# A GNN kernel on one core: GpSimd's descriptor carve-out in SBUF at half its size

## The reference

```python
edge_index = jnp.stack([src, dst])
x = _layernorm(x + _L0_gnn_ref(x, edge_index, edge_attr_4, edge_attr_8, 12500, ...), axis=-1)
x = _layernorm(x + _L1_gnn_ref(x, edge_index, edge_attr_3, ...), axis=-1)
```

## Time and profile before

| | |
|---|---|
| Median of three runs | 19,247.4 us |
| Range of the runs | 19,130.4 to 19,343.0 us |
| Profiled execution, its own time | 19,350.1 us |
| Its span (first to last instruction) | 19,348.1 us |
| Mean granted TensorE clock in it | 0.837 |
| TensorE busy | 15,636.7 us, 81% |
| VectorE busy | 12,827.1 us, 66% |
| GpSimd busy | 10,966.2 us, 57% |
| ScalarE busy | 2,132.7 us, 11% |

### The profile page before, as it was taken

One profiled execution on the slowest core, in us unless ns is written; L12 is line 12 of the kernel. 1 busy time (PEld: TensorE's weight loads), 2 busy tenths in 40 slices (PEclk: granted clock), 3 DMA queues, 4 the chain that ended last, 5 costly groups with the idle time before them and its releaser, 6 DMA issues.

```text
span 19348.1 us, 198105 instructions
## 1 busy us (share of the span) xinstructions
PE 15636.7 (81%) x63343; PEld 8350.6 (43%) x63343; DVE 12827.1 (66%) x19056; ACT 2132.7 (11%) x2833; POOL 10966.2 (57%) x11418
## 2 busy tenths in 40 slices
PE   6788888888897887888887888878887887888876
PEld 3333333333344444444444444444444444444443
DVE  4565566566566666766766677666766676666766
ACT  1111111111111000000000000000000000000001
POOL 5455555555545656665654566656655666665654
PEclk7666677666678999999998999898998999999998
DMA  1000000000001111111111111111111111111111
GB/s 35 13 15 14 15 15 15 14 15 15 14 14 29 20 19 20 20 21 20 21 20 27 20 20 21 20 20 20 21 20 27 20 21 20 21 20 19 21 20 26
DMA packets 918110, 382.41 MB, mean 20 GB/s; under 512 B 645444, under 2 KB 871770, under 8 KB 917790
## 3 DMA queue, kind: packets, MB, share of 16 engines
q0 software_dynamic: 367488, 201.16, 7.7%
q1 hardware_dynamic: 379914, 151.24, 3.3%
q10 hardware_dynamic: 170644, 29.29, 0.8%
HBM read 344.13 MB, written 36.68 MB: 20 GB/s over the span
## 4 chain that ended last, share of the span: by engine, by line
PE 35%; DVE 23%; another core or an unknown queue 20%; issue 18%; POOL 1%; ACT 1%; DMA 0%; DVEq 0%; ACTq 0%; SPq 0%; POOLq 0%
PE ps L1669 16%; PE ps L1566 5%; PE ps L1655 4%; DVE big L1290 3%; PE ps L1582 3%; DVE big L1344 3%; DVE xg L1348 3%; DVE big L1017 2%; DVE big L1335 2%; PE ps L1555 2%; DVE big L1133 2%; PE ps L1549 1%; POOL xg L601 1%; PE ps L1681 1%
## 5 line engine op out<-in xcount | busy, mean ns | idle before, releaser
L601 POOL DMA_INDIRECT xg<-x_rows,idx x8205 | 7886.5, 961 | 5274.4 <-issue 2319.1
L1669 PE MATMUL ps<-xw,big 128*128 128x512 f32 x14112 | 7086.0, 656 | 1640.3 <-DVE big L1344 1420.8
L1669 PEld LDWEIGHTS ps<-xw,big 128*128 128x128 f32 x14112 | 2855.6, 210 | 5150.7 <-issue 3654.6
L601 POOL DMA_INDIRECT xg<-in_x,idx x3125 | 2990.0, 957 | 2760.4 <-DVE big L1101 1785.5
L1344 DVE TENSOR_TENSOR big<-ps,col_hot 128x512 f32<-128x512 f32 x1176 | 810.0, 689 | 3775.2 <-remote 2023.6
L1655 PE MATMUL ps<-big 128*128 128x128 f32 x18816 | 2478.5, 284 | 326.1 <-issue 199.0
L1566 PE MATMUL ps<-w,big 65*128 65x256 f32 x6272 | 2462.8, 534 | 205.1 <-DVE big L1133 187.8
L1655 PEld LDWEIGHTS ps<-big 128*128 128x128 f32 x18816 | 2269.7, 196 | 494.4 <-issue 292.1
L836 ACT COPY big<-ps 128x1024 f32<-128x1024 f32 x1176 | 1189.2, 1013 | 11480.3 <-remote 5734.2
L1566 PEld LDWEIGHTS ps<-w,big 65*128 65x128 f32 x6272 | 1543.8, 264 | 1937.7 <-issue 1593.0
L1065 DVE TENSOR_REDUCE big<-ps 128x32 f32<-128x512 f32 x784 | 539.5, 688 | 1910.7 <-remote 1251.4
(11 more groups left out here) (153 smaller groups left out, 7663.9 us busy)
## 6 DMA issues: line engine op xcount, KB each, us to landing
xg<-x_rows,idx POOLq DMA_INDIRECT x8205
row_of<-pick_rows SPq DMA_DIRECT2D x294, 256.0 KB
xg<-in_x,idx POOLq DMA_INDIRECT x3125
agg_rows<-rts ACTq DMA_DIRECT2D x294, 64.0 KB
meta<-in_coord_t SPq DMA_DIRECT2D x294, 48.0 KB
big<-in_rad SPq DMA_DIRECT2D x196, 64.0 KB
carry<-carry_items SPq DMA_DIRECT2D x392, 32.0 KB
idx<-in_src_t SPq DMA_DIRECT2D x392, 16.0 KB
```

The lines of the kernel that those rows point to most:

```text
L601: return nc.gpsimd.indirect_dma_start(out=dst_tile, out_offset=None, in_=table, in_offset=bass.IndirectOffsetOnAxis(ap=index, axis=0))
L1669: nc.tensor.matmul(ps[:, 6, :], row_hot[:, k, b, :], xw[:, b, :], start=(b == 0), stop=False)
```

## The change

[...]

```diff
--- before.py
+++ after.py
@@ -1825,7 +1825,7 @@
     from concourse.bass_utils import run_bass_kernel_spmd
 
     nodes, edges, data = prepare(inputs)
-    nc = bacc.Bacc("TRN2", target_bir_lowering=False, num_devices=1)
+    nc = bacc.Bacc("TRN2", target_bir_lowering=False, num_devices=1, dynamic_dma_scratch_size=8192)
     arrays, args = {}, {}
     for name, v_ in data.items():
         arrays[f"in_{name}"] = v_
```

## The result

| | before | after |
|---|---|---|
| Median of 6 runs | 19,257.6 us | 20,088.9 us |
| Range | 19,130.4 to 19,344.1 | 20,015.9 to 20,350.5 |
| Profiled execution, its own time | 19,350.1 us | 20,015.9 us |
| Mean granted clock in it | 0.837 | 0.825 |

The ratio of the times is 1.042, with a 95% interval of 1.038 to 1.046. Forecast was 19,247 us, "same" with 0.90. The forecast is wrong.

What follows compares the result with a forecast made beforehand. It took the exchange between TensorE's products and VectorE's multiplications as the path, GpSimd's gathers beside it. All terms were 0: 19,350 us for the profiled execution, 19,247 against the median, range 19,109 to 19,400.

Steps and rivals of the forecast that it cites:

- The long gathers: Gathers above the median, 146 us in all, put to VectorE's accesses; change 0 us, bound +146 us of GpSimd's time.
- gather of 2.9 us: Sign on GpSimd that the forecast is wrong; also what the bursts of the drain rival would show.
- The window totals' median: 21 gathers ending each pass, median 1,027 ns; forecast 0 us, bound 167 us; a move over 0.2 us would refute.
- the forecast's term for the addresses: Tensors at other bases: 21 us either way on VectorE by L1352's spread, 29 us by L1133; 0 in the sum.
- Room: GpSimd's gathers in flight: five at most, two nearly always; half the room holds at least two, so 0 us.
- idle time by issue still 0.30 us each: Sign expected after the change: GpSimd's issue gap between one gather and the next stays 0.30 us.
- most of it inside 8,382 us of idleness: If long gathers were a price of room, the +146 us would fall mostly in GpSimd's idle time.
- most stalls fall into GpSimd's idleness: Why 1 of the drain's 4% was put within 1% and 3 slower by over 1%.
- Drained at each turn: Rival: GpSimd waits for all gathers to land when room is used up; 195 us more, 19,442 us; chance 4%.
- The backlog meets a limit: Rival: gathers stall at window totals and first 76 us; 167 us, or 13,500 more if limited to one; chance 2%.
- The number is not used: Rival: size reaches only the layout, or less was ever used; 19,247 us; 94% shared with ample room.
- A move of the time with GpSimd's rows as before and another mean clock would be scatter: Closing rule for reading the result: such a move would not count as an effect of the change.

Runs made afterwards that it cites:

- `pad` alone: Kernel before with its room unchanged, plus an unused tensor of 2,048 floats laid out first: 15,450.7 us, 1.0003.
- room for 56: The changed kernel, 8,192 bytes, counted in gathers: 1.042 against the kernel before, 1.0652 in a later set.
- room for 57: Kernel before with 8,320 bytes and an unused tensor of 2,016 floats laid out first: 19,220.6 us, 0.9948.
- the quarter of the room: Kernel before with 4,096 bytes: 20,535.8 us, 1.0649 on a slower chip; with an unused 3,072-float tensor, 1.0018 on a faster one.
- the late start by hand: Kernel before, full room, three more semaphore increments behind each GpSimd wait: 21,180.4 us, 1.0947 on a slower chip; 15,447.0 us, 1.0002 on a faster one.

## Why the prediction was wrong, point by point

**Right:** the instructions and their order, 11,414 gathers with a median of 947 ns, 367,488 packets, few gathers in flight (at the end of each gather of the first pass at most 4 have not landed, before and after). The long gathers are those on VectorE's scans: in the layers all 119 of over 1.5 us before, and all 143 after, overlap one of L1042. In the layers no gather of 2.9 us turned up, the longest being 1.94 us; but there are more long ones after (147 of over 1.5 us against 123), so "the change leaves these be" is off by 35 us of GpSimd's time in the layers. The window totals' median is 1,023 ns against 1,027. `pad` alone cost nothing with the full room (1.0003). No run shows the forecast's term for the addresses, nor the 21 us that it gives the range: no trace holds an address, and the runs show `pad` alone. L1133 and L1352 last 547 and 1,224 ns in the median, as the prediction said.

**The step that failed** is *Room*: "If room had to be won back from landed gathers, ... it costs nothing that these rows can show. Cost: 0 us." The rows it rested on were durations of gathers, and the cost does not lie in a duration. It lies in the idle time ahead of a gather. The sign that the prediction itself had named, "idle time by issue still 0.30 us each", did show it: it is 0.75 us each after (8,469.2 us in 11,297). That the room has to be won back at a price was to be seen in the trace of before: in the first pass the 114th gather and every 64th behind it pay 0.83 us, 48 in all, and 31 more do in the layers. From GpSimd's timeline at 326 us:

```profile
326.19 0.94 POOL L601 DMA_INDIRECT xg<-in_x,idx  x1 [10.54 <-DVE big L1101]
328.26 0.94 POOL L601 DMA_INDIRECT xg<-in_x,idx  x1 [1.13 <-issue]
329.51 0.95 POOL L601 DMA_INDIRECT xg<-in_x,idx  x1 [0.30 <-issue]
```

1.13 us of `issue` where 0.30 is the rule. The changed kernel has no such gather in the flow. Instead nearly every gather behind a wait of over 1.2 us is late, such as the first of these:

```profile
318.94 0.95 POOL L601 DMA_INDIRECT xg<-in_x,idx  x1 [10.36 <-issue]
320.19 0.95 POOL L601 DMA_INDIRECT xg<-in_x,idx  x1 [0.30 <-issue]
321.44 0.94 POOL L601 DMA_INDIRECT xg<-in_x,idx  x1 [0.30 <-issue]
```

That GpSimd looks at its room only now and then, and pays for the look, and that with room for 56 the look falls on the gathers behind waits, is my guess from the 0.83 us at every 64th gather and the 0.27 us behind the waits; no run here shows the look itself. The prediction took the size of the room for a limit on what is in flight, asked whether 2 to 5 fit, and had that right. The room also has a turn of its own (112 gathers with 16,256 bytes), and how it falls among the waits was not asked.

**The second step that failed** was the cover: "most of it inside 8,382 us of idleness", said of the long gathers, and "most stalls fall into GpSimd's idleness", said of the drain. The idle time of GpSimd was no cover: with the full room and 0.235 us of delay the kernel was 9.5% slower. Yet the loss is not in waits for gathers. VectorE's waits for a gather's rows (L1344) rise from 73.0 us in 18 to 125.0 us in 32. That is 52 us; 549 of the 666 us are VectorE's idle time behind the recorded end of TensorE's one-hot products, the `remote` of L1344, which the prediction did not look at. Of the stage row's mean clock of 0.91 the forecast made nothing. It was the average of 215 steps at one price and 73 at another, 9 us apart, and that a small shift could move steps from one kind to the other was in none of the terms.

**The rivals.** *Drained at each turn* had the right object, a price for each turn of the room that depends on its size, and put it at a landing of 1.99 us for 98 more turns, 195 us. Its own test, bursts with gathers of 2.9 us, was the wrong place to look. As written it is refuted: the delay is 0.27 us behind nearly every wait and not a landing once in a turn, and room for 57, with twice the turns of the full room by the estimate of 57 gathers and 113, costs nothing (0.9948). *The backlog meets a limit* is refuted by the quarter of the room: it should cost more than half does, and costs the same, 1.0649 against 1.0652, and the window totals' median did not rise. *The number is not used* is refuted by the late starts.

"A move of the time with GpSimd's rows as before and another mean clock would be scatter" was no safe rule either. GpSimd's durations and counts are as before, only its waits differ, and the clock is 0.825 against 0.837; the two sets of runs do not overlap: the slowest before is 19,344 us, the fastest after 20,016.

**What stays open:** by which wait a gather that is 0.27 us late comes to more long steps, since few waits of VectorE are for gathers; what TensorE does between the recorded end of a one-hot product and its semaphore, and whether the lower clock is a cause of the long steps or follows from their idle time; why the late start by hand costs more than half the room on a slower chip, and less on a faster one; why 8,192 bytes delay nearly every long wait and 4,096 only those of the layers, 8,320, 12,288, the default or 24,576 none of them steadily, and 16,256 one in nine of the layers' and one in six of the first pass's, and much longer. Also open is why the first comparison gave 4.2% and the second 6.5% for the same kernel; the long steps, 135 and 198, go with it, but what sets their number on a given chip was not found.

**The better version** is the one with 8,320 bytes: it asks for about half the bytes of the default, by the estimate of 16,256 to 16,546, at no loss of time. That a tensor can have the rest was not shown: the run has a `pad` there. Its 0.9948 (0.9912 to 0.9983) against the kernel before comes from one comparison and is a gain of half a per cent at best. Besides the late starts it does not have the gap of 0.83 us at every 64th gather of the first pass; that this makes the 0.5% is not shown.

## What to carry to other kernels

When a change touches how a queue is fed, read the idle time ahead of its instructions and the time from the release to the start, not only their durations; here 1,785.5 us of waits named L1101 turned into `issue` when the start came 0.29 us later behind the release. When a stage's mean clock lies below 1 (here 0.91), cut it into its steps before calling a sub-microsecond shift free: if the steps are of two kinds, a shift can cost by how many more are long (here 135 for 73). Look up what a large `remote` wait (here 2,023.6 us) stands for before trusting the named ones. And a size that holds a whole number of the program's groups is worth trying one unit larger, as 8,320 bytes for 8,192 here.

## What the runs showed of the hardware that was not expected

- The first gather behind a wait starts 0.75 us behind the release, or 1.02 us, by 128 bytes of `dynamic_dma_scratch_size` (8,320 or 8,192), in the layers. With 16,256 bytes one wait in nine there is 1.58 us late, and one in six of the first pass 1.41.
- With the default the 114th gather of the first pass and every 64th behind it cost 0.83 us more (1.13 against 0.30 us).
- The same kernel took 15,450 us on some chips and 19,300 on others, at mean clocks of 0.925 and 0.837. A late start of 0.235 us cost 9.5% on the second kind and 0.02% (-0.07 to 0.12) on the first.
- Leaving waits out, with gathers then earlier, made the kernel 5.6% slower on the second kind of chip (1.0558), and changed nothing that the interval shows on the first (0.9995, 0.9985 to 1.0004; with the full room, where the 5.6% is for room for 57).
- On the slower chips the semaphore of a TensorE product comes up to 11 us behind the recorded end of its last matmul; VectorE stands idle for 1,539 us of such time before, 2,087 after, and for 25 us on a faster chip.
